# Moving the rank counts, the value copies and the last projections of a routing stage to other places in five queues

## What is computed

```python
x = x + mlstm(layernorm(x), ctx, ctx)
n = layernorm(x)
shared = (silu(n @ sw1) * (n @ sw3)) @ sw2
logits = n @ router_w.T + experts_bias
rw, sel = top_k(logits, 2); rw = softmax(rw)
x = x + shared + sum(rw[k] * expert[sel[k]](n) for k in range(2))
x = x + attention(layernorm(x), keys = ctx @ Wk.T + bk, values = ctx @ Wv.T + bv)
x = x + ffn_of_8_experts(layernorm(x))
```

## Time and profile before

| | us |
|---|---|
| median of 3 runs | 1169.76 (1168.09 to 1171.35) |
| the profiled execution, own time | 1156.03 |
| its span, first to last instruction | 1154.0 |
| TensorE busy | 957.6 (83%) |
| VectorE, ScalarE, GpSimd busy | 734.0, 534.4, 507.2 |
| granted TensorE clock, mean | 0.883 |

### The profile page before, as it was taken

The page is one execution under the profiler, slowest core; times in us unless marked ns, Lnnn a source line. Parts: engine busy times, 40 slices in busy tenths (PEclk is TensorE's granted clock), DMA queues, the critical chain, the costliest instruction groups (busy, mean ns, idle before and its releaser), DMA issues. The chain is left out here.

```text
span 1154.0 us, 24802 instructions
## 1 busy us (share of the span) xinstructions
PE 957.6 (83%) x9121; PEld 684.5 (59%) x9121; DVE 734.0 (64%) x2271; ACT 534.4 (46%) x848; POOL 507.2 (44%) x566
## 2 busy tenths in 40 slices
PE   6819998665777766999997279899899899989998
PEld 1217776444555543666665157777777778856665
DVE  7776999765566652878776455555566656345553
ACT  2457886422333322676665234445455455323231
POOL 4302675676566660555554765434544521011110
PEclk9959998886778767999999569988989989989999
DMA  8554553321222234233332211111111310024331
GB/s 258 196 156 137 160 164 108 122 95 51 60 60 67 63 99 126 96 126 120 120 125 80 62 36 39 39 29 29 47 38 32 88 43 20 21 69 109 95 92 36
DMA packets 84598, 101.28 MB, mean 88 GB/s; under 512 B 36128, under 2 KB 57312, under 8 KB 83712
## 3 DMA queue, kind: packets, MB, share of 16 engines
q1 hardware_dynamic: 56576, 78.20, 22.2%
q0 software_dynamic: 8192, 16.79, 5.0%
q10 hardware_dynamic: 19712, 4.72, 2.5%
HBM read 64.81 MB, written 30.67 MB: 83 GB/s over the span
## 5 line engine op out<-in xcount | busy, mean ns | idle before, releaser
L1701 ACT ACTIVATE split_table<-attn_psT 128x1024 f32<-128x1024 f32 x64 | 65.5, 1024 | 163.9 <-DMA early_ctxT<-in_ctxT 94.1
L1022 POOL TENSOR_TENSOR moe_h_lo<-moe_hid,moe_h_hi 128x512 f16<-128x512 f32 x78 | 90.6, 1163 | 103.3 <-ACT moe_h_hi L1175 98.4
L1169 ACT ACTIVATE moe_act_g<-moe_psG,split_unscale 128x512 f32<-128x512 f32 x110 | 75.5, 687 | 66.5 <-PE moe_psU L1104 32.4
L1279 DVE SCALAR_TENSOR_TENSOR moe_hid<-moe_psU,split_to_hidden,moe_act_g 128x512 f32<-128x512 f32 x110 | 81.0, 748 | 37.8 <-ACT moe_act_g L1169 37.7
L1592 PE MATMUL attn_psO<-heads_vheads,split_table 128*64 128x18 f32 x2048 | 81.8, 214 | 24.9 <-issue 24.8
L1592 PEld LDWEIGHTS attn_psO<-heads_vheads,split_table 128*64 128x64 f32 x2048 | 72.7, 140 | 37.0 <-issue 35.7
L1764 DVE TENSOR_REDUCE split_table<-attn_psN 128x16 f32<-128x1024 f32 x62 | 75.7, 1221 | 17.0 <-PE attn_psN L1555 9.0
L1175 ACT ACTIVATE moe_h_hi<-moe_hid 128x512 f16<-128x512 f32 x110 | 68.4, 622 | 35.0 <-DVE moe_hid L1279 17.6
L1016 POOL DMA_INDIRECT scratch_xs<-cell_xn,res_row x64 | 63.1, 986 | 41.5 <-DVE res_row L1273 24.3
L1788 DVE RECIPROCAL split_table<-attn_psO 128x16 f32<-128x16 f32 x64 | 16.5, 257 | 101.8 <-PE attn_psO L1592 66.1
L1016 POOL DMA_INDIRECT scratch_xs<-moe_xn,res_row x64 | 63.2, 987 | 38.3 <-DVE res_row L1273 20.8
(11 more groups left out here) (282 smaller groups left out, 2788.7 us busy)
## 6 DMA issues: line engine op xcount, KB each, us to landing
early_ctxT<-in_keys SPq DMA_DIRECT2D x16, 512.0 KB, 3.6
scratch_ys<-cell_h SPq DMA_DIRECT2D x26, 256.0 KB, 2.0
early_ctxT<-in_values SPq DMA_DIRECT2D x8, 544.0 KB, 3.7
mlstm_vals<-in_values SPq DMA_DIRECT2D x8, 544.0 KB, 4.0
res_x<-in_x SPq DMA_DIRECT2D x16, 256.0 KB, 6.2
early_ctxT<-in_ctxT SPq DMA_DIRECT2D x16, 256.0 KB, 6.3
attn_in_ctxT<-attn_in_ctxT ACTq DMA_DIRECT2D x64, 64.0 KB
scratch_x<-split_table SPq DMA_DIRECT2D x16, 256.0 KB
```

The costliest lines, as they stand in the source:

```text
L1022: pool.tensor_tensor(h_lo[u % 3][c][:, :], hid[u % 2][c][:, :], h_hi[u % 3][c][:, :], ALU.subtract).then_inc(lo_done[c], 1)
L1169: act.activation(act_g[c][:, :], psG[c][:, :], ACT.Silu, scale=sw.unscale[:, 0:1]).then_inc(silu_done, 1)
L1279: v.scalar_tensor_tensor(out=hid[u % 2][c][:, :], in0=psU[c][:, :], scalar=sw.to_hidden[:, 0:1], in1=act_g[c][:, :], op0=ALU.mult, op1=ALU ...
L1701: act.activation(probT[i % 2][:, :, :, :, :].rearrange("p r b m q -> p (r b m q)"), psT[:, :], ACT.Exp).then_inc(prob_done, 1)
```

## The change

Five things. `count_(g)` goes from behind `down` to the head of TensorE's round, and `route` now also waits for the rows of the group before. `place_(g)` goes to the head of VectorE's round. The DMAs that rearrange the values go from ScalarE's to SyncE's queue. Three of the eight tail clears go from SyncE's to ScalarE's queue. At the seam, the last group's key and value projections move behind the first slot tile's transposition and matmuls, `low_x(GROUPS)` goes ahead of `add`, the last part of `map_tiles` becomes `find_slots` and runs in slot tile u = 20, and tanh and `shares` go to the end of the stage.

```diff
+        def move_values(eng, g):
+            staged, final = (... for n in (g + 1, g))
+            eng.wait_ge(v_raw, ONE + g + 1)
+            eng.wait_ge(v_moved, ONE + 16 * 4 * g)
+            for b2 in range(2):
+                for half in range(2):
+                    eng.dma_start(final[...], staged[...]).then_inc(v_moved, 16)
...
         def _(sp):
+            for g in range(GROUPS - AHEAD):
+                move_values(sp, g)
             sp.wait_ge(tails_done, ONE + 1)
-            for e in range(E0):
+            for e in range(E0 - ACT_TAILS):
...
             for j in range(NB - 1):
                 load(j)
+            for g in range(GROUPS - AHEAD, GROUPS - 1):
+                move_values(sp, g)
             for j in range(SLOT_TILES):
                 if j + NB - 1 < SLOT_TILES:
                     load(j + NB - 1)
+                if j == 0:
+                    move_values(sp, GROUPS - 1)
                 store(j)
...
             def route(g):
                 pe.wait_ge(x_hi_done, ONE + g + 1)
                 pe.wait_ge(either_done, ONE + g)
+                pe.wait_ge(placed, ONE + g)
...
             for g in range(GROUPS):
+                count_(g)
                 if g + 1 < GROUPS:
                     turn(g + 1)
                 up(g)
...
                     down(g - 2)
-                count_(g)
                 if g >= AHEAD:
                     project_v(g - AHEAD)
             total()
-            for g in range(GROUPS - AHEAD, GROUPS):
+            for g in range(GROUPS - AHEAD, GROUPS - 1):
                 project_k(g)
-                if g >= GROUPS - 2:
+                if g == GROUPS - 2:
                     down(g)
                 project_v(g)
             turn(GROUPS)
+            project_k(GROUPS - 1)
+            down(GROUPS - 1)
             for u in range(GROUPS, UNITS):
...
                 up(u)
+                if u == GROUPS:
+                    project_v(GROUPS - 1)
...
         def _(act):
-            for g in range(GROUPS - AHEAD, GROUPS):
+            for g in range(GROUPS - AHEAD, GROUPS - 1):
                 k_out(g)
                 v_out(g)
-            act.wait_ge(gap_done, ONE + GROUPS)
-            act.activation(tanh[:, :], gap[:, :], ACT.Tanh, scale=0.5).then_inc(tanh_done, 1)
+                if g == GROUPS - AHEAD:
+                    act.wait_ge(blank_done, ONE + 1)
+                    act.wait_ge(tails_done, ONE + 1)
+                    for e in range(E0 - ACT_TAILS, E0):
+                        clear_tail(act, e)
             xT_out(GROUPS)
+            k_out(GROUPS - 1)
...
         def _(v):
             for g in range(GROUPS):
+                place_(g)
                 if g + 1 < GROUPS:
                     low_x(g + 1)
...
                     normalise(g + 2)
-                place_(g)
                 ins = carry(g)
...
             map_tiles()
             add(GROUPS - 2)
-            add(GROUPS - 1)
-            shares()
             v.wait_ge(map_done, ONE + 1)
             weights_of(0)
+            low_x(GROUPS)
+            add(GROUPS - 1)
             weights_of(1)
-            low_x(GROUPS)
             for u in range(GROUPS, UNITS):
...
+                if u == GROUPS + AHEAD:
+                    find_slots()
             y_out_(UNITS - 2)
             y_out_(UNITS - 1)
+            shares()
```

More of the change, by code:

```diff
@@ L914, in phase_moe @@
     UNITS = GROUPS + SLOT_TILES
-    NB, NW, AHEAD = 6, 4, 4
+    NB, NW, AHEAD, ACT_TAILS = 6, 4, 4, 3
     with ExitStack() as ctx:
@@ L968, in group, with clear_tail @@
             return slice(g * TILES, (g + 1) * TILES)
+        def clear_tail(eng, e):
+            tail = eng.value_load(tails[0:1, e:e + 1], min_val=0, max_val=E0 * REGION - GROUP)
+            eng.dma_start(s["xs"][bass.ds(tail, GROUP), :].rearrange("(p t) d -> p t d", p=P), y[0][:, :, :]).then_inc(tails_in, 16)
+        def move_values(eng, g):
+            staged, final = (given.ctxT[:, n * GROUP:(n + 1) * GROUP].rearrange("p (t n c) -> p t n c", t=TILES, n=2) for n in (g + 1, g))
+            eng.wait_ge(v_raw, ONE + g + 1)
+            eng.wait_ge(v_moved, ONE + 16 * 4 * g)
+            for b2 in range(2):
+                for half in range(2):
+                    eng.dma_start(final[half * S:(half + 1) * S, :, b2, :], staged[b2 * S:(b2 + 1) * S, :, half, :]).then_inc(v_moved, 16)
         @block.sync
@@ L977, in _ @@
             sp.dma_start(s["xs"][E0 * REGION:SLOT_ROWS, :].rearrange("(p t) d -> p t d", p=P), y[0][:, :, :]).then_inc(tails_in, 16)
+            for g in range(GROUPS - AHEAD):
+                move_values(sp, g)
             sp.wait_ge(tails_done, ONE + 1)
-            for e in range(E0):
-                tail = sp.value_load(tails[0:1, e:e + 1], min_val=0, max_val=E0 * REGION - GROUP)
-                sp.dma_start(s["xs"][bass.ds(tail, GROUP), :].rearrange("(p t) d -> p t d", p=P), y[0][:, :, :]).then_inc(tails_in, 16)
+            for e in range(E0 - ACT_TAILS):
+                clear_tail(sp, e)
             sp.wait_ge(map_done, ONE + 1)
@@ L1181, in v_out @@
             def v_out(g):
-                staged, final = (given.ctxT[:, n * GROUP:(n + 1) * GROUP].rearrange("p (t n c) -> p t n c", t=TILES, n=2) for n in (g + 1, g))
                 act.wait_ge(v_full, ONE + g + 1)
                 act.activation(given.ctxT[:, (g + 1) * GROUP:(g + 2) * GROUP], psKV[:, :], ACT.Copy).then_inc(v_raw, 1)
[L1185 to L1189, removed]
             xT_out(0)
@@ L1220, in _ @@
                 high_part(u, 0)
+                if u == GROUPS:
+                    v_out(GROUPS - 1)
             high_part(UNITS - 1, 1)
+            act.wait_ge(gap_done, ONE + GROUPS)
+            act.activation(tanh[:, :], gap[:, :], ACT.Tanh, scale=0.5).then_inc(tanh_done, 1)
             act.wait_ge(v_moved, ONE + 16 * 4 * GROUPS)
@@ L1324, in map_tiles, with find_slots @@
                 v.tensor_scalar(rows[:, :], first_row[:, :], float(E0 * REGION), None, ALU.min).then_inc(map_done, 1)
+            def find_slots():
                 step(v.tensor_tensor(shift[:, :], ends[:, :], tiles[:, :], ALU.subtract))
```

## The result

The changed kernel takes 1217.26 us (median of 6 runs, 1213.77 to 1219.28), the kernel before 1169.18 beside it: ratio **1.045**, 95% interval 1.041 to 1.050. Forecast was 1144.

| us | before | after | difference | forecast |
|---|---|---|---|---|
| end of `choose(0)` | 222.4 | 220.9 | -1.5 | |
| 15 rounds, to the end of `choose(15)` | 187.9 | 242.0 | +54.1 | -13.4 |
| seam, to the first slot `up` | 42.9 | 38.0 | -4.9 | -14.5 |
| slot tiles, to the end of the last `down` | 175.3 | 174.6 | -0.7 | +2.5 |
| attention and last layer | 525.4 | 542.0 | +16.6 | 0 |

A forecast was written before the change was run, and what follows sets the result against it. It took the rounds to be bound by a loop through late counts signal, `place_`, `choose`, ScalarE wait, `add` and `down`, GpSimd no bound; -13.4 - 14.5 + 2.5 = -25.4 from 1169.8 gives 1144 us, range 1135 to 1180.

The forecast's parts named there:

- the signal came 2.8 us after the work: Steady rounds before the change: VectorE idle 2.86 us before `rank`, the counts' signal arriving 2.8 us late, no cause known.
- signal and counts: First term of the new loop from one `choose` to the next, put at 0.3 us.
- Counts and ranks first: Group rounds: counts no longer behind `down`, new loop 11.5 us a round; `choose(15)` ends 13.4 us earlier.
- The chain of 11.5 us: New loop between ends of `choose` at 2.4 GHz; terms sum to 11.4, taken as 11.5.
- rival B: Rounds: TensorE's clock stays at 1.2 GHz, rounds of 13.2 us, total 1172, no change; chance 0.14.
- Rival A: Rounds: TensorE's signals held until a burst of scatters is over, 15.5 us a round, total 1192; chance 0.22.
- 0.15 us after `rank`, so the delay is once a round: Argument against rival A: in steady rounds ScalarE's copy followed `rank` by 0.15 us, so delay is not per signal.
- Value DMAs: Rounds: moved to SyncE, ScalarE loses 2.63 us a round; no further gain, but had they stayed, loop 14.1.
- Seam: From end of `choose(15)` to first slot `up`: 28.4 us where it was 42.9, so -14.5.
- Three clears fewer in a row: Seam: five clears instead of eight on SyncE, 1.5 us each; named among what gave most of -14.5.
- Moved work: Slot tiles: value projection 1.1 us and `find_slots` 1.4 us added, together +2.5.

The follow-up runs named there:

- m4: Changed kernel with four scatters a group instead of eight; 15 rounds 176.1 us, steady round 11.6, seam 29.5.
- m13: Changed kernel with seven GpSimd subtractions and one scatter in place of a group's eight scatters; 15 rounds 230.5 us, steady round 14.8 to 16.4.
- m1: Kernel before with only counts and ranks moved, and route's added wait; 15 rounds 270.0 us, ratio 1.087.
- m10: Kernel of m2 with the value DMAs back on ScalarE's queue; ratio 0.996 to the kernel before.
- m2: Changed kernel with counts and ranks back in their old places; ratio 0.986 to the kernel before.
- m11: Kernel of m2 with all eight tail clears on SyncE's queue; median 1153.56 us, kernel before 1169.06.

## Why the prediction was wrong

- **What bounds the kernel.** The step that failed first: "the signal came 2.8 us after the work" was taken as a fixed delay, once a round, and the new loop's sum put "signal and counts" at 0.3 us and the signals of the transposition and of `up` at nothing. In the changed kernel they came 2.6 to 5.9 us after the work (the table and the semaphore events above). The prediction's own rows gave the loop: `rank` to first scatter 1.19, burst 9.88, signal 1.78 after its end, sum 12.85, the whole round. GpSimd's burst was in the loop before, and with 10.2 us it was called no bound. m4 (half the burst, 11.6) shows how much of a round hangs on it.
- **Counts and ranks first, -13.4.** It came as +54.1 less 1.5. Of the 67.5 us between forecast and result in the rounds, 56.6 are the eleven rounds 4 to 14 (16.6 a round where 11.5 were put) and 9.2 are round 3. The chain of 11.5 us was about right (11.6 with half the scatters), but more of it lies behind a held signal. Before, a held signal released `rank` and the burst was 1.19 us away. Now it releases ScalarE's copies: from 302.28 to `low_part` at 304.98 are 2.70, and then `add` and `rank` come as well. Rounds 0 to 2, in which no `down` stands ahead of `route`, took 12.4 to 13.1 where they took 8.2 to 8.8, at a granted clock of 0.62 from 214 to 255 us (0.86 before): rival B in small, as far as the forecast of 13.2 at the lower clock shows it. The prediction read the 187.9 us as 12.5 a round and saw neither these short rounds nor round 3, which it put at 11.5 like the rest. Round 3 took 21.2 and takes 20.7, because GpSimd computes `cell_next_rstd` for the groups to come between the first two bursts and then issues sixteen scatters without a pause (246.82 to 267.07; before, 243.08 to 263.28).
- **Rival A happened**, with a chance of 0.22. Its mechanism was right; its size was not. 15.5 a round had `gate` released at once; ScalarE does the two copies of the transposition and the value copy first (302.28 to 303.73), which adds 1.3 to 1.5 us, and the round was 16.8. Its time of 1192 also had three quick rounds. The argument against it, "0.15 us after `rank`, so the delay is once a round", read the end of one hold as a single delay: all signals held came out together.
- The rule weighed in the prediction, of the Trainium skill's "SBUF — State Buffer", section "Who interferes with whom" (TensorE and ScalarE never wait on anyone there), was no ground against A. What was late here was mostly the signal, with the work done; late in the burst matmuls of TensorE waited too (299.15 to 299.86), and the trace does not say for what. m13 agrees with what the same section says of the other two, that GpSimd and VectorE can block each other: the normalisation went from 1.11 to 3.85 us.
- **Value DMAs.** Worth 2.8 us a round only in the new order (m1 against the changed kernel), nothing in the old one (m10: 189.0, m2: 189.2 and 189.6), where the prediction had listed them in the loop.
- **Seam, -14.5.** It came as -4.9. The sum was near (29.5 with prompt signals in m4, 28.4 put). What it lacked was the held signal ahead of `low_part` and `add`: the last burst began 5.2 us late, the load was issued 6.9 late, and the projections took 2.8 more. "Three clears fewer in a row", one of the three reasons given for the gain, is worth nothing that shows (m11).
- **Moved work, +2.5.** -0.7: nothing of either shows in the slot tiles' time.

## What to carry to other kernels

When a wait's releaser is not named, add up the loop through the other engines before calling the wait a constant: a sum equal to the period is the bound. Moving a step earlier in one queue can put a late signal in front of more work; find out which signal is late and what stands behind it in the new order. Here bursts of indirect DMAs should be paced so that what others wait for comes early in them, and the bulk of the matmuls after.

## What the runs showed of the hardware

In the changed kernel's steady rounds TensorE's signals came up to 5.9 us after their matmuls while GpSimd issued eight indirect DMAs in a row, and an idle ScalarE took one 4.6 us late; most came in a bundle 1.5 to 1.9 us after the burst. Early in a burst, and with a GpSimd that only computes, takers had them within 0.04 us. ScalarE's signals in the same rounds all came 0.01 us after their work. Up to 14 matmuls into a burst signals were prompt, from 26 on nearly all were late, and the pace of the matmuls counts as well. What stands behind it was not settled, nor whether the recording of the profile has a part in it.
